# Last feed-forward layer of a four-layer network: dense products ahead of the routing, four batches held in SBUF, one output transfer per batch

## The chip, the cores and the metric

The kernel runs on one core of a Trainium2 chip. The metric is the time of one execution on the device, in microseconds (us); lower is better. The network is one program of four layers (attention, cross-attention, feed-forward in each); the change touches the last sublayer, the store of the result behind it, and nothing else that is computed.

## What is computed

The input is x, 8 batches of 100 tokens of 256 numbers, in fp32. Each of twelve sublayers adds its result to x. The last one is a feed-forward layer with a router:

```python
    def _L3_ffn_ref(x, Wg, bg, We, be):
        probs = jax.nn.softmax(x @ Wg + bg, axis=-1)
        idx = jnp.argmax(probs, axis=-1)
        p = jnp.take_along_axis(probs, idx[..., None], axis=-1)[..., 0]
        e_idx = idx % We.shape[0]
        h = jax.nn.relu(jnp.einsum('bsd,edf->besf', x, We) + be[None, :, None, :])
        onehot = jax.nn.one_hot(e_idx, We.shape[0], dtype=x.dtype)
        out = jnp.einsum('besf,bse->bsf', h, onehot) * p[..., None]
        return out
    x = x + _L3_ffn_ref(_layernorm(x, axis=-1), L3_ffn_Wg, L3_ffn_bg, L3_ffn_We, L3_ffn_be)
```

Wg is 256 by 256, We is 8 experts of 256 by 256, be is 8 by 256. Every token goes through all 8 experts, and one of the 8 results is kept, times the router's probability p.

## The kernel before

The engines run from instruction streams of their own, joined by semaphores. A sublayer is one such block. Behind each stands a barrier of all engines (`end_sublayer`), and nothing of the next begins before it. x stays in SBUF as 100 partitions by 8 batches by 256.

The last sublayer is `l3_ffn`. Its parts, in the order in which they depend on each other:

- The sync engine (SP) issues five loads (L81): `wg`, `bg`, `be`, `iota`, and last `we`, which is 2 MB. All count on one semaphore, `loaded`, and TensorE and VectorE wait for the whole of it.
- VectorE takes the layer norm's statistics (`norm_stats_vector`, L88 to L95) and writes the normed batches `xn` (L106). TensorE meanwhile runs 18 dummy products (`keep_busy`, L113), turns the batches (L3605), and ScalarE copies them to `xt` (L3642). `by_pairs` runs this over two slots, the first pair written out and the other three in a loop on registers.
- Gates: TensorE multiplies each of 8 batches by `wg` (L3615) into two PSUM regions of `summed` in turn. VectorE adds `bg` (L3665), takes the maximum (L3667) and negates it (L3669). ScalarE takes the exponential and its sum (L3648).
- Routing: when all 8 batches are through, VectorE takes the peaks (L3672), their places (L3675), p (L3676, L3679), the expert's number (L3678, L3681) and the one-hot rows `hot` (L3683).
- Dense product: per batch, TensorE fills the four banks of `wide` (L3626), each with two experts' results. The bank of batch b waits until VectorE has read that of batch b - 1 (`z_read`). Batch 0's four banks are filled ahead of the routing. Then TensorE turns `hot` (L3631), ScalarE copies it (L3650), and a small product with `be` gives each token its expert's bias in `summed` (L3634 for batch 0, L3621 for the others).
- Choice: VectorE copies the bias to `acc` (L3689), adds each of 8 experts' results times its one-hot number, each step waiting for the one before (L3694), applies the relu and p (L3700) and adds to x (L3702).

Then follow the barrier and `store` (L247 to L250), one transfer of 800 KB from x to the output.

## Time and profile before

| what | us |
|---|---|
| median of 3 runs | 1530.92 |
| lowest and highest of them | 1526.48, 1542.85 |
| span of the profiled execution | 1546.3 |
| of it, from the start of the last sublayer | 98.6 |

The span runs from the first to the last instruction; for the profiled execution no other time than this span is given. It is longer than each of the three runs, so the differences below are read inside the span and then taken over to the median. PE is TensorE (PEld its weight loads), DVE is VectorE, ACT is ScalarE. A row of the waits says how long an engine stood and who let it go. PEclk, or the granted clock, is 1.0 at 2.4 GHz and 0.5 at 1.2 GHz.

### The profile page before, as it was taken

What the parts mean: (1) busy time and instruction counts of PE and PEld (TensorE: products, weight loads), DVE (VectorE), ACT (ScalarE), POOL (GpSimd) and SP (SyncE); (2) the same over time, 40 slices, a digit from 0 to 9 for tenths busy, and PEclk for the clock granted to TensorE, in tenths of its full rate; (3) what the DMA queues carried; (4) which work ended last, traced back from release to release, by engine and by line L of the source; (5) the groups of instructions that cost most, each with busy time, mean ns of one, the idle gap of its engine ahead of it and who ended that gap; (6) DMA issues with size and microseconds to landing.
All of it is one profiled execution on the core that took longest, in us unless ns stands there. A gap on an engine that the chain in (4) does not pass through costs nothing. (4 is left out here: it accounts for less than half of the span.)

```text
span 1546.3 us, 31598 instructions
## 1 busy us (share of the span) xinstructions
PE 1394.0 (90%) x12524; PEld 1073.6 (69%) x12524; DVE 780.3 (50%) x1747; ACT 640.6 (41%) x1680; POOL 184.2 (12%) x194
## 2 busy tenths in 40 slices
PE   7999999999989899989999768999976896799887
PEld 6776668766556687759999655669974575588632
DVE  3666577665656676500000366610127485477665
ACT  3443226633367266224444235532224684166300
POOL 3000250000034200131111200040023000300000
PEclk9999999999999999999999877999997997799999
DMA  6000240011301200557994100174311000700100
GB/s 209 2 1 1 67 73 10 3 43 40 77 12 20 48 3 3 172 197 262 338 349 172 34 1 22 57 305 150 131 42 53 1 2 1 112 6 3 66 0 22
DMA packets 43944, 120.20 MB, mean 78 GB/s; under 512 B 11931, under 2 KB 28440, under 8 KB 38412
## 3 DMA queue, kind: packets, MB, share of 16 engines
q1 hardware_dynamic: 33048, 62.04, 14.0%
q0 software_dynamic: 7616, 53.12, 9.9%
q10 hardware_dynamic: 3136, 3.03, 0.7%
q8 instruction: 101, 1.65, 0.4%
q14 instruction: 43, 0.35, 0.1%
HBM read 95.78 MB, written 11.00 MB: 69 GB/s over the span
## 5 line engine op out<-in xcount | busy, mean ns | idle before, releaser
L798 PE MATMUL wide<-early_kt,early_q 32*100 32x361 f32 x512 | 107.4, 506 | 2.8 <-PEq L66 1.6
L2528 ACT ACTIVATE l1f_hidden<-wide,l1f_pack 128x128 f32<-128x128 f32 x160 | 58.8, 368 | 78.0 <-PE wide L2467 68.1
L113 PE MATMUL summed<-ident 128*128 128x128 f32 x338 | 51.7, 322 | 37.8 <-PEq L66 37.8
L2630 DVE TENSOR_TENSOR l1f_out<-summed,l1f_pack 128x256 f32<-128x256 f32 x20 | 8.5, 424 | 152.8 <-PE summed L2475 152.8
L113 PEld LDWEIGHTS summed<-ident 128*128 128x128 f32 x338 | 49.1, 234 | 45.3 <-issue 45.3
L2467 PEld LDWEIGHTS wide<-l1f_rt,l1f_pack 128*128 128x128 f32 x640 | 74.5, 192 | 1.8 <-issue 0.8
L2467 PE MATMUL wide<-l1f_rt,l1f_pack 128*128 128x128 f32 x640 | 74.8, 275 | 0.6 <-ACT l1f_rt L2518 0.6
L2475 PE MATMUL summed<-l1f_pack,l1f_hidden 128*128 128x256 f32 x320 | 72.4, 379 | 0.0
L1194 DVE TENSOR_REDUCE l3x_mx<-wide 100x2 f32<-100x722 f32 x64 | 57.8, 907 | 16.5 <-PE wide L798 16.5
L1194 DVE TENSOR_REDUCE l1x_mx<-wide 100x2 f32<-100x722 f32 x64 | 57.8, 907 | 14.0 <-PE wide L798 14.0
L2475 PEld LDWEIGHTS summed<-l1f_pack,l1f_hidden 128*128 128x128 f32 x320 | 59.2, 190 | 7.2
L1194 DVE TENSOR_REDUCE l0x_mx<-wide 100x2 f32<-100x722 f32 x64 | 57.8, 907 | 11.4 <-PE wide L798 11.4
L798 PE MATMUL wide<-late_kt,late_q 32*100 32x361 f32 x256 | 57.3, 540 | 3.7 <-DMA late_q<-l3x_both 3.7
L3626 PE MATMUL wide<-l3f_we,l3f_xt 128*100 128x512 f32 x128 | 59.5, 620 | 1.2 <-DVE l3f_acc L3694 1.2
L2382 POOL DMA_INDIRECT l1f_pack<-l1f_pack_dram,l1f_packi x20 | 18.9, 946 | 255.1 <-DVE l1f_out L2630 129.1
L2973 PE MATMUL wide<-l2f_rt,l2f_w 128*128 128x200 f32 x256 | 46.4, 341 | 0.8 <-ACT l2f_rt L3010 0.8
L3020 ACT ACTIVATE l2f_hidden<-wide 128x200 f32<-128x200 f32 x64 | 21.6, 338 | 61.2 <-PE wide L2973 61.2
L3626 PEld LDWEIGHTS wide<-l3f_we,l3f_xt 128*100 128x100 f32 x128 | 21.7, 174 | 35.1 <-issue 32.2
L2973 PEld LDWEIGHTS wide<-l2f_rt,l2f_w 128*128 128x128 f32 x256 | 45.1, 196 | 1.0 <-issue 1.0
L798 PEld LDWEIGHTS wide<-early_kt,early_q 32*100 32x100 f32 x512 | 32.0, 160 | 19.5 <-issue 10.6
L2951 PE MATMUL summed<-l2f_hidden,l2f_w 128*128 128x200 f32 x256 | 44.8, 333 | 0.0
L1004 ACT ACTIVATE l3x_pt<-turned 121x300 f32<-121x300 f32 x64 | 26.9, 424 | 41.7 <-PE turned L813 41.7
(595 smaller groups left out, 3370.9 us busy)
## 6 DMA issues: line engine op xcount, KB each, us to landing
l2f_w<-l2f_w_dram SPq DMA_DIRECT2D x16, 1024.0 KB, 11.7
ctxt<-ctxt_dram SPq DMA_DIRECT2D x4, 1083.0 KB, 17.3
early_kt<-soon_kd SPq DMA_DIRECT2D x32, 90.8 KB, 3.2
l1f_sorted_x<-l1f_zeros SPq DMA_DIRECT2D x4, 640.0 KB
l1f_rows<-l1f_sorted_x SPq DMA_DIRECT2D x20, 128.0 KB, 7.6
l1f_sorted_y<-l1f_out ACTq DMA_DIRECT2D x20, 128.0 KB
l0f_w<-l0f_w_dram SPq DMA_DIRECT2D x18, 128.0 KB, 2.1
l1f_shared<-l1f_shared_dram SPq DMA_DIRECT2D x1, 2180.0 KB, 8.5
```

The source lines that it names most:

```text
L113: pe.matmul(net.summed[:, 1, 0:P], net.ident[:], net.ident[:], start=True, stop=True)
L798: pe.matmul(wide[0:S, i, 0:SKV], q4[R * i:R * (i + 1), g % 2, b, g // 2, :], kt[R * i:R * (i + 1), g % 2, b, g // 2, 0:SKV], start=True, s ...
L1004: act.activation(pt[:, h % 8], scored[j][0:CH, 0:NCH * S].rearrange("s (c t) -> s c t", c=NCH), ACT.Exp).then_inc(sem["p_ready"], 1)
L1194: dve.tensor_reduce(mx[:, n % 2, :].rearrange("s (i r) -> s i r", r=R)[:, 2 * pair:2 * pair + 2, 0:1], wide[0:S, 2 * pair:2 * pair + 2, 0: ...
L2382: pool.indirect_dma_start(out=pack[:, n % SLOTS, :], out_offset=None, in_=dram["l1f_pack"], in_offset=bass.IndirectOffsetOnAxis(ap=packi[: ...
L2467: last = pe.matmul(wide[:, f % 4, 0:P], w1_of(w, k, f), rt[:, n % 2, k, :], start=k == 0, stop=k == KC - 1)
L2475: last = pe.matmul(summed[:, n % 2, 0:E], hidden[:, f, 0:P], w2_of(w, f), start=f == 0, stop=f == FC - 1)
L2528: act.activation(hidden[:, f, 0:P], wide[:, f % 4, 0:P], ACT.Gelu, bias=b1_of(pack[:, n % SLOTS, :], f)).then_inc(sem["h_ready"], 1)
L2951: last = pe.matmul(summed[:, 0, m * CR:(m + 1) * CR], w2[:, e % SLOTS, f, m * P:(m + 1) * P], hidden[:, f, :], start=f == 0, stop=f == FC - 1)
L2973: last = pe.matmul(wide[:, f % 4, 0:CR], w1[:, e % SLOTS, k, f * P:(f + 1) * P], rt[:, e % 2, k, :], start=k == 0, stop=k == KC - 1)
L3020: act.activation(hidden[:, f, :], wide[:, f % 4, 0:CR], ACT.Gelu).then_inc(sem["h_ready"], 1)
L3626: last = pe.matmul(wide[0:S, n, :], xt[:, k, b, :], we[:, k, n * 512:(n + 1) * 512], start=k == 0, stop=k == KC - 1)
```

## The change

- Loads: SP issues `wg`, `bg`, `we`, and then `iota` and `be`, with a semaphore for each use in place of one for all.
- `xn` has a place for every batch, and the loops on registers are written out. The gates of batches 0 and 1 stand between the turns of x. The gates use four PSUM regions (two of `summed`, two of `turned`). ScalarE loads the table of the exponential before it copies `xt`.
- TensorE goes on from the gates straight into the dense product. Batches 0 to 3 (`HELD`) are copied by ScalarE from `wide` to `held` in SBUF (`hold`), and a bank is free again when it is copied (`z_held`). Batches 4 to 7 are read from PSUM by VectorE as before. The turn of `hot` stands inside batch 1, the bias products inside batches 1 and 2 and then behind each batch; ScalarE copies each bias to `bias`.
- VectorE multiplies `hot` by p once. Each batch is summed in two accumulators (even and odd experts), and these are joined. The relu and the addition to x are one instruction. The bias goes in with the second step; for batch 0 it is added at the end.
- Each batch's x is sent out by SP in a transfer of its own, 100 KB, as soon as it is done; `store` is gone.
- SBUF of the sublayers before (`given`, `late`) is given back ahead of the last one.

```diff
-def store(net):
-    nc = net.nc
-    stored = net.sem("stored")
-    with nc.Block() as block:
-        @block.sync
-        def _(sp):
-            sp.dma_start(net.dram["out"].rearrange("b s d -> s b d"), net.x[:]).then_inc(stored, 16)
-            sp.wait_ge(stored, 16)
...
+    HELD = 4
...
-        pairs = [(wg[:], dram["l3f_wg"]), (bg[:], dram["l3f_bg"].partition_broadcast(S)),
-                 (be[:], dram["l3f_be"]), (iota[:], dram["iota8"]), (we[:], dram["l3f_we"])]
-        n_loaded = 16 * len(pairs)
-        xn = sb("xn", [S, 2, E])
+        xn = sb("xn", [S, B, E])
...
+        held = sb("held", [S, HELD, NE, E])
+        bias = sb("bias", [S, 2, E])
+        acc = sb("acc", [S, 2, 2, E])
...
+        gates = (summed[0:S, 0, 0:E], summed[0:S, 1, 0:E], turned[0:S, 0, 0:E], turned[0:S, 1, 0:E])
...
-                load_weights(sp, net, pairs, sem["loaded"])
+                load_weights(sp, net, [(wg[:], dram["l3f_wg"])], sem["wg_loaded"])
+                load_weights(sp, net, [(bg[:], dram["l3f_bg"].partition_broadcast(S))], sem["bg_loaded"])
+                load_weights(sp, net, [(we[:], dram["l3f_we"])], sem["we_loaded"])
+                load_weights(sp, net, [(iota[:], dram["iota8"]), (be[:], dram["l3f_be"])], sem["be_loaded"])
+                for b in range(B):
+                    sp.wait_ge(sem["x_done"], b + 1)
+                    sp.dma_start(dram["out"][b], net.x[:, b, :]).then_inc(sem["stored"], 16)
+                sp.wait_ge(sem["stored"], 16 * B)
...
+                def gate(b):
+                    pe.wait_ge(sem["xt_ready"], B if b in (2, 3) else b + 1)
+                    if b >= 4:
+                        pe.wait_ge(sem["lg_ready"], b - 3)
+                    for k in range(KC):
+                        last = pe.matmul(gates[b % 4], xt[:, k, b, :], wg[:, k, :], start=k == 0, stop=k == KC - 1)
+                    last.then_inc(sem["g_psum"], 1)
+                def layer(b, n):
+                    u = b * BANKS + n
+                    if b >= 1:
+                        if b <= HELD:
+                            pe.wait_ge(sem["z_held"], u - BANKS + 1)
+                        else:
+                            pe.wait_ge(sem["z_read"], u - BANKS * (HELD + 1) + 1)
+                    for k in range(KC):
+                        last = pe.matmul(wide[0:S, n, :], xt[:, k, b, :], we[:, k, n * 512:(n + 1) * 512], start=k == 0, stop=k == KC - 1)
+                    last.then_inc(sem["z_psum"], 1)
...
+                def shift(b):
+                    if b == 0:
+                        pe.wait_ge(sem["be_loaded"], 32)
+                        pe.wait_ge(sem["ht_ready"], 1)
...
+                        pe.wait_ge(sem["b_ready"], b - 1)
+                    pe.matmul(summed[0:S, b % 2, 0:E], hot_t[:, b, :], be[:], start=True, stop=True).then_inc(sem["b_psum"], 1)
+                for b in range(B):
+                    turn_x(b)
+                    if b == 1:
+                        pe.wait_ge(sem["wg_loaded"], 16)
+                    if b in (2, 4):
+                        gate(b // 2 - 1)
+                for b in range(2, B):
+                    gate(b)
+                pe.wait_ge(sem["we_loaded"], 16)
+                for b in range(B):
                     for n in range(BANKS):
-                        if b >= 1:
-                            pe.wait_ge(sem["z_read"], (b - 1) * BANKS + n + 1)
-                        for k in range(KC):
-                            last = pe.matmul(wide[0:S, n, :], xt[:, k, b, :], we[:, k, n * 512:(n + 1) * 512], start=k == 0, stop=k == KC - 1)
-                        last.then_inc(sem["z_psum"], 1)
-                    if b == 0:
-                        pe.wait_ge(sem["hot_ready"], 1)
-                        for c in range(B):
-                            last = pe.transpose(turned[0:NE, c // 4, (c % 4) * S:(c % 4 + 1) * S], hot[:, c, :], net.ident[0:S, 0:S])
-                        last.then_inc(sem["ht_psum"], 1)
-                        pe.wait_ge(sem["ht_ready"], 1)
-                        pe.matmul(summed[0:S, 0, 0:E], hot_t[:, 0, :], be[:], start=True, stop=True).then_inc(sem["b_psum"], 1)
+                        layer(b, n)
+                        if b == 1 and n == 2:
+                            turn_hot()
+                        if b == 1 and n == 3:
+                            shift(0)
+                        if b == 2 and n == 0:
+                            shift(1)
+                        if b == 2 and n == 2:
+                            shift(2)
+                        if 2 <= b < B - 1 and n == BANKS - 1:
+                            shift(b + 1)
...
+                act.preload_act_table(ACT.Exp)
...
+                def hold(b, n):
+                    act.wait_ge(sem["z_psum"], b * BANKS + n + 1)
+                    act.activation(held[:, b, 2 * n:2 * n + 2, :].rearrange("s e d -> s (e d)"), wide[0:S, n, :], ACT.Copy).then_inc(sem["z_held"], 1)
+                def copy_bias(b):
+                    act.wait_ge(sem["b_psum"], b + 1)
+                    if b >= 2:
+                        act.wait_ge(sem["b_taken"], b - 1)
+                    act.activation(bias[:, b % 2, :], summed[0:S, b % 2, 0:E], ACT.Copy).then_inc(sem["b_ready"], 1)
+                for b in range(B):
+                    copy_xt(b)
+                for b in range(B):
+                    exps(b)
+                for b in range(HELD):
+                    for n in range(BANKS):
+                        hold(b, n)
+                        if b == 1 and n == 2:
+                            act.wait_ge(sem["ht_psum"], 1)
+                            act.activation(hot_t[:].rearrange("e (a b) s -> e a (b s)", a=2), turned[0:NE, :, 0:4 * S], ACT.Copy).then_inc(sem["ht_ready"], 1)
+                        if b == 1 and n == 3:
+                            copy_bias(0)
+                        if b == 2 and n == 0:
+                            copy_bias(1)
+                        if b == 3 and n == 0:
+                            copy_bias(2)
+                for b in range(3, B):
+                    copy_bias(b)
...
-                def normal(b, slot, first):
-                    if not first:
-                        dve.wait_ge(sem["xt_psum"], b - 1)
-                    normalise(dve, net, xn[:, slot, :], b).then_inc(sem["xn_ready"], 1)
-
-                by_pairs(dve, B, normal)
-                dve.wait_ge(sem["loaded"], n_loaded)
+                for b in range(B):
+                    normalise(dve, net, xn[:, b, :], b).then_inc(sem["xn_ready"], 1)
+                dve.wait_ge(sem["bg_loaded"], 16)
                 for b in range(B):
                     dve.wait_ge(sem["g_psum"], b + 1)
-                    dve.tensor_tensor(lg[:, b, :], summed[0:S, b % 2, 0:E], bg[:], ALU.add).then_inc(sem["lg_ready"], 1)
+                    dve.tensor_tensor(lg[:, b, :], gates[b % 4], bg[:], ALU.add).then_inc(sem["lg_ready"], 1)
...
+                dve.wait_ge(sem["be_loaded"], 32)
+                dve.drain()
+                dve.tensor_tensor(hot[:], expert[:].broadcast_to([S, B, NE]), iota[:], ALU.is_equal)
+                dve.drain()
+                dve.tensor_tensor(hot[:], hot[:], p[:].broadcast_to([S, B, NE]), ALU.mult).then_inc(sem["hot_ready"], 1)
+                dve.drain()
+                def expert_of(b, e):
+                    return held[:, b, e, :] if b < HELD else wide[0:S, e // 2, (e % 2) * E:(e % 2 + 1) * E]
+                def choose(b):
+                    one = acc[:, b % 2]
+                    for n in range(BANKS):
+                        if n >= 1:
+                            dve.drain()
+                        if b < HELD:
+                            dve.wait_ge(sem["z_held"], b * BANKS + n + 1)
+                        else:
+                            dve.wait_ge(sem["z_psum"], b * BANKS + n + 1)
+                        for r in range(2):
+                            e = 2 * n + r
+                            if n == 0 and (r == 0 or b == 0):
+                                last = dve.tensor_scalar(one[:, r, :], expert_of(b, e), hot[:, b, e:e + 1], None, ALU.mult)
+                            elif n == 0:
+                                dve.wait_ge(sem["b_ready"], b + 1)
+                                last = dve.scalar_tensor_tensor(out=one[:, r, :], in0=expert_of(b, e), scalar=hot[:, b, e:e + 1],
+                                                                in1=bias[:, b % 2, :], op0=ALU.mult, op1=ALU.add)
+                            else:
+                                last = dve.scalar_tensor_tensor(out=one[:, r, :], in0=expert_of(b, e), scalar=hot[:, b, e:e + 1],
+                                                                in1=one[:, r, :], op0=ALU.mult, op1=ALU.add)
+                        if b >= HELD:
                             last.then_inc(sem["z_read"], 1)
                     dve.drain()
-                    dve.tensor_scalar(one, one, 0.0, p[:, bass.ds(b, 1), :].rearrange("s o e -> s (o e)"), ALU.max, ALU.mult)
+                    if b == 0:
+                        dve.wait_ge(sem["b_ready"], 1)
+                        dve.tensor_tensor(one[:, 1, :], one[:, 1, :], bias[:, 0, :], ALU.add)
+                        dve.drain()
+                    dve.tensor_tensor(one[:, 0, :], one[:, 0, :], one[:, 1, :], ALU.add).then_inc(sem["b_taken"], 1)
                     dve.drain()
-                    dve.tensor_tensor(net.x[:, b, :], net.x[:, b, :], one, ALU.add)
-
-                by_pairs(dve, B, choose)
+                    dve.scalar_tensor_tensor(out=net.x[:, b, :], in0=one[:, 0, :], scalar=0.0, in1=net.x[:, b, :],
+                                             op0=ALU.max, op1=ALU.add).then_inc(sem["x_done"], 1)
+                for b in range(B):
+                    choose(b)
...
-        net.given = Given(net, ctx, "given")
-        with ExitStack() as again:
-            net.context = Context(net, again, "ctxt3")
-            l2_ffn(net)
-        l3_attn(net)
-        net.tiles = RowTiles(net, ctx, "late")
-        cross_attn16(net, "l3x", fresh=True)
+        with ExitStack() as third:
+            net.given = Given(net, third, "given")
+            with ExitStack() as again:
+                net.context = Context(net, again, "ctxt3")
+                l2_ffn(net)
+            l3_attn(net)
+            net.tiles = RowTiles(net, third, "late")
+            cross_attn16(net, "l3x", fresh=True)
         l3_ffn(net)
-        store(net)
```

The lines of the changed kernel are numbered anew: L3612 is the gate, L3623 the dense product, L3639 the bias product, L3679 the copy to `held`, L3685 that to `bias`. On TensorE, this is the stage before, from the turns of x on:

```order
L3605 MATMUL turned<-ident,l3f_xn 128x100 x2
L121 REGISTER_ALU
L121 COMPARE_AND_BRANCH
L3615 MATMUL summed<-l3f_wg,l3f_xt 100x256 x16
L3626 MATMUL wide<-l3f_we,l3f_xt 100x512 x8
L3631 MATMUL turned<-ident,l3f_hot 8x100 x8
L3634 MATMUL summed<-l3f_be,l3f_hot_t 100x256
L3621 MATMUL summed<-l3f_be,l3f_hot_t 100x256
L3626 MATMUL wide<-l3f_we,l3f_xt 100x512 x8
```

And this is the same stretch of TensorE's stream in the changed kernel:

```order
L3604 MATMUL turned<-ident,l3f_xn 128x100 x6
L3612 MATMUL summed<-l3f_wg,l3f_xt 100x256 x2
L3604 MATMUL turned<-ident,l3f_xn 128x100 x4
L3612 MATMUL summed<-l3f_wg,l3f_xt 100x256 x2
L3604 MATMUL turned<-ident,l3f_xn 128x100 x6
L3612 MATMUL turned<-l3f_wg,l3f_xt 100x256 x4
L3612 MATMUL summed<-l3f_wg,l3f_xt 100x256 x4
L3612 MATMUL turned<-l3f_wg,l3f_xt 100x256 x4
L3623 MATMUL wide<-l3f_we,l3f_xt 100x512 x14
L3630 MATMUL turned<-ident,l3f_hot 8x100 x8
L3623 MATMUL wide<-l3f_we,l3f_xt 100x512 x2
L3639 MATMUL summed<-l3f_be,l3f_hot_t 100x256
```

The turn of `hot` stood behind 8 products of the dense layer and now stands behind 14, that is, behind three banks of batch 1 (two products fill a bank). The first bias product stands a bank further on.

On ScalarE, the end of the sublayer was this (`l3f_ex` is the exponential, `l3f_hot_t` the turned one-hot rows):

```order
L3648 ACT_TABLE_LOAD
L3648 ACTIVATE l3f_ex,l3f_sm<-l3f_lg,l3f_ntop 100x256 x8
L3650 ACTIVATE l3f_hot_t<-turned 8x800
```

And it is now this:

```order
L3675 ACTIVATE l3f_ex,l3f_sm<-l3f_lg,l3f_ntop 100x256 x8
L3679 ACTIVATE l3f_held<-wide 100x512 x7
L3696 ACTIVATE l3f_hot_t<-turned 8x800
L3679 ACTIVATE l3f_held<-wide 100x512
L3685 ACTIVATE l3f_bias<-summed 100x256
L3679 ACTIVATE l3f_held<-wide 100x512
L3685 ACTIVATE l3f_bias<-summed 100x256
```

Sixteen copies to `held` and eight to `bias` are new; seven of the sixteen stand ahead of the copy of the turned `hot`, and all of them behind the eight exponentials.

## Rows read from the trace of the kernel before

**Rows 1.** Stretches: us, busy us of each engine, granted clock, DMA share, GB/s.
```profile
0.00:1447.70 1447.70, 1311.90 (x12288) 1036.02 (x12288) 719.19 (x1580) 629.86 (x1652) 184.25 (x194) 0.95 0.26 81
1447.70:1546.30 98.60, 82.09 (x236) 37.58 (x236) 61.15 (x167) 10.71 (x28) 0.00 (x0) 0.90 0.10 34
```
**Rows 2.** Chain that ended last: start, us, what.
```profile
1449.18 8.63 DMA l3f_we<-l3f_we_dram
...
1457.85 4.54 PE summed L3615 x12
...
1478.09 0.69 PE summed L3634 x2
...
1480.41 9.85 PE wide L3626 x16
1490.26 0.60 PE summed L3621 x2
1490.86 7.04 PE wide L3626 x16
...
1529.07 7.05 PE wide L3626 x16
...
1538.08 0.42 DVE x L3702
```
**Rows 3.** Timeline of the last sublayer: start, us, engine, line, instruction, idle before.
```profile
1447.76 2.71 DVE L88 BATCH_NORM_STATS2 stats<-x 100x6 f32<-100x256 f32 x8 [1.15 <-PEq L66]
...
1453.86 0.57 ACT L3642 ACTIVATE l3f_xt<-turned 128x200 f32<-128x200 f32 x2 [2.17 <-PE turned L3605]
...
1466.58 1.08 PE L3615 MATMUL summed<-l3f_wg,l3f_xt 128*100 128x256 f32 x4 [0.36 <-DVE l3f_lg L3665]
...
1467.10 0.41 DVE L3665 TENSOR_TENSOR l3f_lg<-summed,l3f_bg 100x256 f32<-100x256 f32 x1
...
1467.49 7.03 PE L3626 MATMUL wide<-l3f_we,l3f_xt 128*100 128x512 f32 x16
...
1468.18 0.41 DVE L3665 TENSOR_TENSOR l3f_lg<-summed,l3f_bg 100x256 f32<-100x256 f32 x1
...
1476.04 0.23 DVE L3683 TENSOR_TENSOR l3f_hot<-l3f_expert,l3f_iota 100x64 f32<-100x64 f32 x1
...
1476.32 0.85 PE L3631 MATMUL turned<-ident,l3f_hot 100*8 100x100 f32 x8 [1.80 <-DVE l3f_hot L3683]
1477.21 0.83 ACT L3650 ACTIVATE l3f_hot_t<-turned 8x800 f32<-8x800 f32 x1 [7.23 <-PE turned L3631]
...
1539.65 0.31 SPq L250 DMA_DIRECT2D out_dram<-x  x1
```
**Rows 4.** Stretches of 1 us, columns as in rows 1.
```profile
1461.00:1462.00 1.00, 1.00 (x4) 0.66 (x3) 0.82 (x3) 0.08 (x1) 0.00 (x0) 0.50 0.00 0
1462.00:1463.00 1.00, 1.00 (x6) 0.71 (x5) 0.57 (x3) 0.60 (x2) 0.00 (x0) 0.97 0.00 0
...
1480.00:1481.00 1.00, 0.59 (x1) 0.41 (x2) 0.84 (x2) 0.00 (x0) 0.00 (x0) 0.50 0.00 0
...
1486.00:1487.00 1.00, 1.00 (x3) 0.34 (x2) 0.31 (x2) 0.00 (x0) 0.00 (x0) 1.00 0.00 0
```
**Rows 5.** Groups by form: instruction, count, busy us, mean ns, idle before.
```profile
L457 ACT ACTIVATE l0a_v<-wide 100x512 f32<-100x512 f32 x10 | 6.0, 597 | 6.6 <-PE wide L372 6.6
...
L3694 DVE SCALAR_TENSOR_TENSOR l3f_acc<-wide,l3f_hot,l3f_acc 100x256 f32<-100x256 f32 x64 | 30.9, 483 | 16.9 <-PE wide L3626 9.5 <-issue 6.3
L3094 DVE SCALAR_TENSOR_TENSOR x<-l2f_back,l2f_prob,x 100x256 f32<-100x256 f32 x16 | 7.7, 484 | 18.0 <-DMA l2f_back<-sorted_y,l2f_placei 18.0
```
**Rows 6.** Waits of SP's queue: engine, line, releaser, us, times, longest.
```profile
SPq L247 <- DMA out_dram<-x: 5.9, 1, 5.9
```
**Rows 7.** DMA issues: transfer, engine, count, KB each, us to landing.
```profile
early_q<-soon_qt SPq DMA_DIRECT2D x8, 50.0 KB, 2.2
...
early_q<-soon_qt SPq DMA_DIRECT2D x8, 12.5 KB, 1.8
```

More of the change, by code:

```diff
@@ new lines, in turn_hot @@
+                def turn_hot():
+                    pe.wait_ge(sem["hot_ready"], 1)
+                    pe.wait_ge(sem["lg_ready"], B)
+                    for c in range(B):
+                        last = pe.transpose(turned[0:NE, c // 4, (c % 4) * S:(c % 4 + 1) * S], hot[:, c, :], net.ident[0:S, 0:S])
+                    last.then_inc(sem["ht_psum"], 1)
+                def shift(b):
+                    if b == 0:
+                        pe.wait_ge(sem["be_loaded"], 32)
+                        pe.wait_ge(sem["ht_ready"], 1)
+                    if b >= 2:
+                        pe.wait_ge(sem["b_ready"], b - 1)
+                    pe.matmul(summed[0:S, b % 2, 0:E], hot_t[:, b, :], be[:], start=True, stop=True).then_inc(sem["b_psum"], 1)
@@ L3645, in _, with exps @@
[L3645 to L3646 removed]
+                    act.activation(xt[:, :, b, :], turned[:, b % 2, 0:KC * S].rearrange("p (k s) -> p k s", k=KC), ACT.Copy).then_inc(sem["xt_ready"], 1)
+                def exps(b):
                     act.wait_ge(sem["top_ready"], b + 1)
                     act.activation(ex[:, b, :], lg[:, b, :], ACT.Exp, bias=ntop[:, b, :], accum_out=sm[:, b, :]).then_inc(sem["ex_ready"], 1)
[L3649 removed]
```

44 lines of the change are left out of this document (6 added, 38 removed).

## The prediction

> **What bounds the kernel now.** I read the stretches first. The last sublayer and the store take 98.6 us of the 1546.3 us span [rows 1]; the 1447.7 us ahead of them run the same instructions in both kernels, so they cancel. Then I read the chain that ended last [rows 2]. It passes from the load of `we` to TensorE, through VectorE's routing, and from 1480.41 to 1536.12 it is TensorE alone: batches of 7.04 us with 0.60 us of bias product between them. So the dense product on TensorE bounds the sublayer, and time is won only where TensorE stands, where it runs at half clock, and ahead of and behind it. The timeline [rows 3] and the clock by microseconds [rows 4] show these places:
>
> - The gates. TensorE starts them at 1457.85, when `we` is in, though the first copies of x are done at 1454.43 (1453.86 + 0.57). The first 12 passes take 4.54 us, 1.51 a batch; a batch at full clock takes 1.08 [rows 2, 3]. The clock is 0.50 at 1461 and back at 0.97 at 1462 [rows 4]. The last gate ends at 1467.66.
> - The routing. Batch 0 ends at 1474.52 (1467.49 + 7.03). Then TensorE stands 1.80 us for `hot`, turns it, stands 0.9 us for ScalarE's copy, does 1.2 us of bias products and stands until 1480.41 for VectorE's first bank. After that the clock is 0.50 until it is 1.00 again at 1486 [rows 4], and batch 1 takes 9.85 us where the next takes 7.04.
> - The end. VectorE is done at 1538.50, SP issues the store at 1539.65 and then stands 5.9 us for it, to 1545.86 [rows 2, 3, 6]. The span ends 0.4 us later.
>
> **The change part by part.**
>
> *Gates ahead.* `wg` no longer waits for `we`, and the gates of batches 0 and 1 stand between the turns. The first can start once two batches are copied and the third is turned, near 1454.6. Two gates (2.16 us) and the next two turns fill TensorE until about 1457.2. Three turns and their copies remain, some 0.45 us each since a copy is 0.29 (0.57 for two), so the six other gates start near 1458.6 and, at 1.08 each, end near 1465.1. That is 2.5 us earlier. VectorE keeps up: it also needs 1.08 a batch (1468.18 less 1467.10 [rows 3]). The bounds: no gain if the gates end where they did; 3.6 us if they follow without any wait. A fall of the clock to half over four gates would cost 4 x 0.43 = 1.7 us of the 2.5. The table load that moved ahead of the copies lies beside the norm's steps, where ScalarE idles 2.17 us before its first copy [rows 3]; if it did not fit there, it would delay the copies by no more than that, 2.2 us.
>
> Of the clock the row says that after the turns, with TensorE waiting on copies, it fell to 0.50. The Trainium skill (TensorE: Matmul & The Clock Gate, Loop structure matters more than you think) says that matmuls kept back to back stay at the full clock, and that copying results out does not break this. By that rule the gates stay at 2.4 GHz and the sum holds; by the row they may still fall. I keep the fall as a rival.
>
> *Dense product without the gap.* From the last gate on TensorE has 8 batches x 7.04, 8 bias products x 0.60 and one turn of `hot` of 0.85: 56.3 + 4.8 + 0.85 = 62.0 us. Before, the same stretch is 1467.66 to 1536.12, 68.5 us. So 6.5 us go, the waits (3.7) and the half clock (2.8), and TensorE ends near 1465.1 + 62.0 = 1527.1. For this, three waits must stay covered:
>
> - Bank free. A copy to `held` of 100 x 512 is like `l0a_v`, 597 ns [rows 5]; a bank is filled in 7.04 / 4 = 1.76. ScalarE starts them after its last exponential, near 1467.4, when one bank is full, and has caught up a bank later. Sixteen copies are 9.6 us beside 28 us of TensorE. If the cover were gone, each copy would cost up to 0.6 us on TensorE.
> - `hot` ready. From the last logits (1468.18) to `hot` (1476.27) are 8.1 us, and the new product with p is one more of 0.23 with its drain, 0.3. With the last logits near 1465.2, `hot` is there at 1473.6. TensorE asks at 1465.1 + 7 banks x 1.76 = 1477.4. The wait of 1.80 is covered by 3.8 us. Queued behind it are all later banks, so each us beyond these 3.8 costs one.
> - ScalarE's copy of the turned `hot` (0.83) lies beside bank (1, 3) of 1.76.
>
> *VectorE's late start.* This is the wait that the change adds. `choose(0)` ends with the bias, which stands behind bank (1, 3) at about 1480.1, the bias product 0.7 and its copy. VectorE has `hot` at 1473.6, is through the eight experts by 1478, stands until about 1481.2, and ends batch 0 at 1482.8. Behind this wait stand batches 1 to 7. A step is 0.48 us by itself, and 0.58 with what it stood by issue ((30.9 + 6.3) / 64 [rows 5]); ten steps a batch are 4.8 to 5.8 us. Reading from SBUF gains nothing: with all operands there a step is 484 ns against 483 from PSUM [rows 5]. I take 4.9, near the lower end, because only every second step now waits for the one before. So batches 1 to 3 are done at 1497.5 (1500.2 at 5.8). TensorE fills (4, 0) at about 1498.9 and needs it read at 1504.8. VectorE has caught up either way, and this part costs nothing.
>
> *The end of the chain.* Behind the last bank stood two steps, the relu and the addition, 2.38 us. Now they are two steps of which one does not wait, the join and the relu with the addition: 2.1, a gain of 0.3 (0 to 0.5).
>
> *The output.* Seven transfers lie beside TensorE's batches, 7.64 us apart. The last is 100 KB. The nearest rows are 1.8 us at 12.5 KB and 2.2 at 50 KB [rows 7], and the 800 KB took 0.31 + 5.9 = 6.2; a line between the last two gives 2.5 at 100 KB. I take 2.2. What stood ahead of the store, the sublayer's barrier, now stands behind it: VectorE's gap at such a seam is 1.15 us [rows 3]. So from VectorE's end to the span's end there are 0.1 + 2.2 + 1.15 = 3.45 us instead of 7.8, a gain of 4.3. Bounds: 5.5 (1.8 us and only the 0.4 of before behind it), and zero (6.2 us and 1.5 behind).
>
> The Trainium skill speaks against this edit (DMA: Bandwidth & Descriptors, Rules for kernel authors): many small transfers should be put together into one large. By its estimate in Anatomy of one DMA, 2.0 us and bytes / 436e3, eight of 100 KB are 17.9 us and one of 800 KB is 3.9. By the sum of all the change would lose; but only the last of the eight is on the chain, 2.2 by that estimate. No row shows a 100 KB store alone.
>
> *Sum.* 2.5 + 6.5 + 0.3 + 4.3 = 13.6 us, so a span of 1532.7. The profiled span, 1546.3, is 1.0% above the median of the runs; the edits do not scale with the rest, so I take 13.6 from the median: 1530.92 - 13.6 = 1517.3, or 0.89% less.
>
> **The rivals.**
>
> 1. *The clock falls in the gates, or the store lands late* (gain 10 to 12). For it: the fall in rows 4 came after turns like these, and no row has the small store. Against: TensorE's waits there shrink. With the fall alone the gain is 13.6 - 1.7 = 11.9; with a transfer of 4 us (midway to 6.2) it is 11.8; with both 10.1. Time 1519 to 1521.
> 2. *All at the good end* (gain 15.8). The gates end 1.1 us earlier and the end takes 2.3 instead of 3.45: 1515.1, just beyond 1%.
> 3. *VectorE becomes the bound*, the one that ends on the other side. Its place is batches 1 to 7, where it reads `held` while ScalarE writes it and SP's transfers read x. It begins at 1482.8 and may end at 1529: 6.6 us a batch before it bounds. From 6.6 + 13.6 / 7 = 8.5 us a batch, 0.85 a step, the kernel is slower than before; to be slower by 1% it takes 10.7. At 1.1 us a step: 7 x 4.4 = 31 us more, a time of 1548. Against it: 484 ns in rows 5.
> 4. *The edit does not advance the gates* (gain 11.1), since the turns go by ScalarE's copies as before and VectorE paces the rest: 1519.8.
>
> **How the numbers follow.** About 1% is what a measurement of this kernel can tell from no change; the three runs lie 1.1% apart. The forecast (gain 12 to 15) has 0.5, rivals 1 and 4 together 0.32, rival 2 has 0.14 and rival 3 0.04. The forecast's 0.89% and the spread of the runs put 0.22 of its 0.5 beyond 1%; rival 2 gives 0.09, rivals 1 and 4 give 0.06. Faster 0.37; slower 0.03, of rival 3; the same 0.60. The range is from 1507 (rival 2 and a median 0.5% low) to 1529 (a gain of 10 and a median 0.5% high).
>
> **What would show it.** In the profile of the changed kernel TensorE's dense product should run without a stand from the last gate on, at a granted clock of 1.00, 62 us long; the clock should not be 0.50 near the turn of `hot`. VectorE should stand once, some 3 us, for ScalarE's bias copy in batch 0, and later only for banks. The last gate should end 17.4 us after the sublayer's start at 1447.7 (before 20.0), and SP should wait about 2 us for the last transfer. The forecast is wrong if TensorE waits for `z_held` or `z_read`, if the whole dense product is longer than 64 us, or if the end from VectorE's last instruction takes over 5 us.

## The result, and the profile of the changed kernel

| | before | changed |
|---|---|---|
| median, 20 runs each, us | 1529.33 | 1515.44 |
| lowest and highest run | 1519.96, 1542.85 | 1506.88, 1529.28 |
| span of the profiled execution | 1546.3 | 1527.5 |
| of it, the last sublayer and the store | 98.6 | 83.0 |

The ratio is 0.9938 with an interval of 0.9914 to 0.9961; the medians stand as 0.9909. The profiled execution of the changed kernel took 1529.28 us around its span of 1527.5. By the bound of 1% this is no change that counts, though the interval lies below 1 altogether. The forecast was 1517.3 us, with 0.60 for within 1%. The 20 runs of the changed kernel lie in two groups, six at 1527.2 to 1529.3 us and fourteen at 1506.9 to 1517.4, and the profiled execution is one of the six.

The stretches of the changed kernel, split where its last sublayer begins (columns as in [rows 1]); the last line is a part of the one above it, from the last gate to the last bank:

```profile
0.00:1444.55 1444.55, 1317.76 (x12288) 1043.97 (x12288) 720.32 (x1580) 630.40 (x1652) 184.49 (x194) 0.94 0.26 81
1444.55:1527.50 82.95, 76.62 (x236) 35.65 (x236) 55.37 (x161) 22.63 (x52) 0.00 (x0) 0.98 0.13 41
...
1460.52:1522.35 61.83, 61.82 (x152) 22.96 (x151) 41.68 (x114) 14.71 (x31) 0.00 (x0) 1.00 0.04 12
```

The last sublayer is 15.6 us shorter, and TensorE is busy for 92% of it instead of 83%. In the dense product it is busy for 61.82 of 61.83 us at a granted clock of 1.00, which is the sign that the prediction named. The other 3.2 us between the two spans lie ahead of it, in instructions that are the same. The chain that ended last shows how it now goes:

```profile
1444.60 5.88 PE summed L113 x36
...
1455.10 1.97 PE turned L3612 x8
1457.07 1.73 PE summed L3612 x8
1458.79 1.73 PE turned L3612 x8
1460.52 12.02 PE wide L3623 x28
1472.54 0.69 PE turned L3630 x8
1473.22 1.72 PE wide L3623 x4
...
1515.30 7.05 PE wide L3623 x16
...
1523.87 0.43 DVE x L3770
```

It is nearly TensorE alone. Where [rows 2] had the load of `we`, VectorE's routing and a batch of 9.85 us, there is now one piece of 12.02 us that runs over the end of batch 0 into batch 1 (28 passes, 0.43 us each, the full clock). The two pieces that the routing fed, VectorE's chain and ScalarE's copy, are gone from the chain. What the engines waited for in this sublayer:

```profile
ACT l3f_held L3679 <- PE wide L3623: 17.3, 14, 1.9
...
DVE l3f_acc L3756 <- ACT l3f_bias L3685: 5.7, 3, 4.4
...
DVE l3f_acc L3766 <- ACT l3f_bias L3685: 2.0, 1, 2.0
```

ScalarE waits for banks and no bank waits for ScalarE. VectorE's new wait for the bias of batch 0 is the 2.0 us; the row above it holds one that the prediction had not seen, 4.4 us in batch 2. And the wait of SP's queue that answers to [rows 6]:

```profile
SPq L3583 <- DMA out_dram<-x: 1.6, 1, 1.6
```

In the table below each profile is cut at four marks. All times are us from the start of the last sublayer (SP's first load of it). "Ahead" is what the profile shows before that, the same instructions in every kernel.

| profile | ahead | last gate ends | from there to the last bank | to VectorE's end | to the span's end | sublayer |
|---|---|---|---|---|---|---|
| before | 1447.7 | 19.95 | 68.45 | 2.39 | 7.80 | 98.6 |
| changed | 1444.6 | 15.97 | 61.82 | 1.96 | 3.20 | 83.0 |
| before, again | 1429.5 | 20.50 | 68.22 | 2.41 | 7.74 | 98.9 |
| changed, again | 1423.6 | 15.12 | 61.83 | 1.96 | 3.21 | 82.1 |
| store alone | 1435.4 | 18.60 | 67.70 | 2.39 | 3.21 | 91.9 |
| one store | 1424.4 | 15.98 | 61.82 | 1.96 | 7.54 | 87.3 |
| gap filled | 1423.2 | 19.81 | 65.90 | 2.40 | 7.83 | 95.9 |
| hot early | 1444.0 | 15.97 | 65.05 | 1.96 | 3.18 | 86.2 |
| semaphores alone | 1421.1 | 18.63 | 67.94 | 2.39 | 7.78 | 96.7 |
| gates behind | 1443.0 | 15.89 | 61.83 | 1.96 | 3.19 | 82.9 |
| two regions | 1424.2 | 17.02 | 61.82 | 1.96 | 3.17 | 84.0 |
| held one | 1443.2 | 15.97 | 65.56 | 1.95 | 3.26 | 86.7 |
| slow choice | 1432.7 | 15.98 | 65.74 | 4.19 | 3.16 | 89.1 |
| fewer dummies | 1444.0 | 15.04 | 61.82 | 1.96 | 3.21 | 82.0 |

### The profile page after: what moved, and what is told of

It is laid out like the page before. It is cut to its first block and busy times, and to the rows that moved or that the text cites. A ratio compares the mean times of both kernels' runs of the same rounds, so it can differ in the third digit from the quotient of the medians.

```text
span 1527.5 us, 31428 instructions
## 1 busy us (share of the span) xinstructions
PE 1394.4 (91%) x12524; PEld 1079.6 (71%) x12524; DVE 775.7 (51%) x1741; ACT 653.0 (43%) x1704; POOL 184.5 (12%) x194
## 5 line engine op out<-in xcount | busy, mean ns | idle before, releaser
L788 PE MATMUL wide<-early_kt,early_q 32*100 32x361 f32 x512 | 112.6, 532 | 2.8 <-PEq L66 1.6
L3623 PE MATMUL wide<-l3f_we,l3f_xt 128*100 128x512 f32 x128 | 57.2, 597 | 0.0
L994 ACT ACTIVATE l1x_pt<-turned 121x300 f32<-121x300 f32 x64 | 26.9, 424 | 40.6 <-PE turned L803 40.6
```

The costliest lines, as they stand in the source:

```text
L788: pe.matmul(wide[0:S, i, 0:SKV], q4[R * i:R * (i + 1), g % 2, b, g // 2, :], kt[R * i:R * (i + 1), g % 2, b, g // 2, 0:SKV], start=True, s ...
L994: act.activation(pt[:, h % 8], scored[j][0:CH, 0:NCH * S].rearrange("s (c t) -> s c t", c=NCH), ACT.Exp).then_inc(sem["p_ready"], 1)
L3623: last = pe.matmul(wide[0:S, n, :], xt[:, k, b, :], we[:, k, n * 512:(n + 1) * 512], start=k == 0, stop=k == KC - 1)
```

## How finely the kernel can be measured, and the two kernels again

Both kernels were run again without an edit.

> The kernel before, unchanged, measured against itself. Both theories: a ratio of 1.000, and its interval and the scatter of its runs say how finely this kernel can be measured. The last sublayer's stretch (from SP's first load of it to the end of the span) takes 98.6 us again within 0.5 us, while the stretch ahead of it varies by several us from one profile to the next.

Measured: 1530.05 us against 1530.10, a ratio of 0.999 (0.9952 to 1.0028), and 98.9 us in the sublayer. The runs of this one kernel lie between 1521.66 and 1546.11 us. The expectation held.

> The changed kernel, unchanged. Theory A (the change acts in the last sublayer alone): that stretch takes 83.0 us again within 0.5 us, 15.6 less than before, and the ratio is about 0.990 with an interval that holds 1 - 15.6/1530 = 0.9898. Rival B (a part of the 15.6 us is given back ahead of the last sublayer, for which the first ratio of 0.9938 speaks): the ratio is 0.993 to 0.995 again, and the stretch ahead of the sublayer is 4 to 6 us longer than in the profiles of the kernel before.

Measured: 1511.54 us (six runs), a ratio of 0.9874 (0.9824 to 0.9924), and 82.1 us in the sublayer. The two ratios of the same kernel, 0.9938 and 0.9874, lie on either side of 1 - 15.6/1530 = 0.9898, and their intervals overlap between 0.9914 and 0.9924. Rival B expected 0.993 to 0.995 and a longer stretch ahead; that stretch was 1423.6 us, shorter than in any but two of the five profiles of the kernel before and its variants. It is not excluded for a part of the gain: the stretch ahead averages 1436.0 us over the nine profiles of the changed kernel and its variants and 1431.4 over the five others, a difference well inside its scatter. That the sublayer was 0.8 us under the expected is its start: here the clock was 1.00 from the first microsecond, while it was 0.50 for some 3.4 us of the dummy products in all the others, and the last gate ended 0.85 us earlier.

The stretch ahead explains the scatter. It ran from 1421.1 to 1447.7 us over 14 profiles of the same instructions. Two profiles of it show one of the places (columns as in [rows 1]). This is the kernel before:

```profile
900.00:960.00 60.00, 44.52 (x203) 29.68 (x204) 41.50 (x109) 26.57 (x59) 0.11 (x1) 0.75 0.05 14
```

And this is the same stretch of "semaphores alone":

```profile
900.00:960.00 60.00, 50.06 (x350) 32.49 (x351) 45.07 (x153) 33.23 (x82) 0.11 (x1) 0.89 0.06 15
```

The granted clock is 0.75 in one and 0.89 in the other, and TensorE gets 203 and 350 instructions done. Against a scatter of 26 us the change's 15.6 are small, so the terms below are read in the sublayer, where the two profiles of each kernel agree within 0.9 us. The kernels behind these terms have one profile each.

## The output

> The kernel before with the output part of the change alone. Theory A: the parts add up, so the stretch from VectorE's last instruction to the end of the span falls from 7.8 to 3.2 us as in the changed kernel, the last sublayer from 98.6 to 94.0, and the ratio is 0.997. Rival C (the small transfers cost something ahead of the end): the dense product or the choice gets longer than before, and less than 4.6 us is won.

```diff
+                for b in range(B):
+                    sp.wait_ge(sem["x_done"], b + 1)
+                    sp.dma_start(dram["out"][b], net.x[:, b, :]).then_inc(sem["stored"], 16)
+                sp.wait_ge(sem["stored"], 16 * B)
...
-                    dve.tensor_tensor(net.x[:, b, :], net.x[:, b, :], one, ALU.add)
+                    dve.tensor_tensor(net.x[:, b, :], net.x[:, b, :], one, ALU.add).then_inc(sem["x_done"], 1)
...
-        store(net)
```

Measured: the end is 3.21 us instead of 7.8, as expected, and so are the waits: 1.6 us for the last transfer, as in the changed kernel. The ratio is 0.9945 (0.9917 to 0.9974), whose interval holds the 0.997 that 4.6 us make. The sublayer is 91.9 us and not 94.0. Rival C is out, since nothing got longer; the other 2.1 us are in the gates (18.60 instead of 19.95) and in the dense product behind them (67.70 instead of 68.45). The clock did not fall in the gates of this profile. It did in the two profiles of the kernel before and in "gap filled", and not in this one and in "semaphores alone", though the gates are the same in all five, and so are the stands of TensorE between the turns ahead of them (0.68, 0.58 and 0.57 us within 0.02). So of the kernel before's sublayer some 1.3 us in the gates, and 2 us with what follows, come and go from one execution to the next.

> The changed kernel with one transfer of 800 KB when all batches are done, in place of eight of 100 KB. Theory A: the wait for the last transfer is the 5.9 us of the kernel before and not 1.6, so the sublayer takes 83.0 + 4.3 = 87.3 us. Rival D (the gain lies in the barrier that stood ahead of the store, not in the size of the transfer): 1.1 us or less is lost, 84.1 us.

```diff
-                for b in range(B):
-                    sp.wait_ge(sem["x_done"], b + 1)
-                    sp.dma_start(dram["out"][b], net.x[:, b, :]).then_inc(sem["stored"], 16)
-                sp.wait_ge(sem["stored"], 16 * B)
+                sp.wait_ge(sem["x_done"], B)
+                sp.dma_start(dram["out"].rearrange("b s d -> s b d"), net.x[:]).then_inc(sem["stored"], 16)
+                sp.wait_ge(sem["stored"], 16)
```

Measured: 87.3 us, to the tenth what theory A said. The wait of SP's queue in this kernel:

```profile
SPq L3583 <- DMA out_dram<-x: 5.9, 1, 5.9
```

It is 5.9 us as in [rows 6]. So 4.3 us come from the size of the last transfer, and rival D is out. The barrier, which only moved from one side of the store to the other, is worth the small rest: 7.54 us at the end here and 7.80 before.

## The gap of the routing, and the half clock behind it

> The kernel before with 17 dummy products on TensorE where it stood for the routing: 8 ahead of the turn of hot, 4 behind it, 5 behind the first bias product. The waits stay. Theory A (the half clock of batch 1 is the price of the gap, 2.8 us, and separate from the gap's 3.8 us): the granted clock stays at 1.00 through batch 1, which takes about 7.1 us instead of 9.85, and the sublayer takes 98.6 - 2.8 = 95.8 us. Rival E (the clock falls there whatever TensorE does): no change, 98.6.

```diff
+                def fill(count):
+                    for _ in range(count):
+                        pe.matmul(summed[:, 1, 256:256 + P], net.ident[:], net.ident[:], start=True, stop=True)
...
                     if b == 0:
+                        pe.wait_ge(sem["lg_ready"], B)
+                        fill(8)
                         pe.wait_ge(sem["hot_ready"], 1)
...
                         last.then_inc(sem["ht_psum"], 1)
+                        fill(4)
                         pe.wait_ge(sem["ht_ready"], 1)
...
+                        fill(5)
```

Measured: 95.9 us in the sublayer. Its chain behind the last gate:

```profile
1442.97 6.87 PE wide L3629 x16
1449.83 1.78 PE summed L3602 x16
...
1451.63 0.85 PE turned L3636 x8
1452.48 0.92 PE summed L3602 x8
1453.40 0.67 PE summed L3640 x2
1454.07 1.31 PE summed L3602 x10
1455.38 0.60 PE summed L3624 x2
1455.98 7.04 PE wide L3629 x16
```

L3602 are the dummies. Batch 1 begins 13.0 us behind the last gate (1442.97 to 1455.98), 12.8 before (1467.66 to 1480.41 [rows 2, 3]), so the gap is all there. But the batch takes 7.04 us and not 9.85, and the granted clock is 1.00 from the last gate on. The half clock is 2.8 us by itself, and it comes from TensorE's stands in the gap, since it is gone when they are filled. Rival E is out.

> The changed kernel with the turn of hot back behind batch 0, so that TensorE waits for the routing again, but not for ScalarE's copy nor for VectorE's first bank. Theory A: batch 0 ends 7.0 us behind the last gate, hot is there 2.9 us later, so TensorE stands 2.9 us, and the sublayer takes 83.0 + 2.9 = 85.9 us if the clock holds. Rival F (any stand of this size drops the clock): 2.8 us more, 88.7.

```diff
-                        if b == 1 and n == 2:
+                        if b == 0 and n == 3:
                             turn_hot()
```

(and the same place for ScalarE's copy of the turned `hot`.) Measured: 86.2 us. TensorE's wait in this kernel:

```profile
PE turned L3630 <- DVE l3f_hot L3735: 3.1, 1, 3.1
```

It stood 3.1 us in one piece, and the clock stayed at 1.00. So rival F is out for this stand. But the length of a stand does not decide: in "store alone" the clock fell behind one of 1.79 us, at the end of `hot`'s turn:

```profile
1462.65 0.85 PE L3635 MATMUL turned<-ident,l3f_hot 100*8 100x100 f32 x8 [1.79 <-DVE l3f_hot L3687]
```

```profile
1463.00:1464.00 1.00, 0.50 (x6) 0.26 (x3) 0.00 (x0) 0.46 (x1) 0.00 (x0) 0.74 0.00 0
1464.00:1465.00 1.00, 0.58 (x2) 0.44 (x3) 0.00 (x0) 0.36 (x1) 0.00 (x0) 0.50 0.00 0
```

In "semaphores alone" it fell half a microsecond later, with the same stand ahead of it. In both profiles of the kernel before it fell behind the second stand, of 0.9 us, and ahead of the third. What decides is not shown. The 3.2 us that this edit costs are what the later place of the turn is worth.

## The gates

> The kernel before with a semaphore for each load and the loads in the new order, but the gates behind all turns as before. Theory A (the gates are won by standing between the turns, so that TensorE is busy and its clock holds): the gates start at most 0.3 us earlier, since the last turn ends when we lands, the clock falls as before, and 0.3 us or less is won. Rival G (they are won by no longer waiting for we): 2 us or more.

```diff
-                load_weights(sp, net, pairs, sem["loaded"])
+                load_weights(sp, net, [(wg[:], dram["l3f_wg"])], sem["wg_loaded"])
+                load_weights(sp, net, [(bg[:], dram["l3f_bg"].partition_broadcast(S))], sem["bg_loaded"])
+                load_weights(sp, net, [(we[:], dram["l3f_we"])], sem["we_loaded"])
+                load_weights(sp, net, [(iota[:], dram["iota8"]), (be[:], dram["l3f_be"])], sem["be_loaded"])
...
-                pe.wait_ge(sem["loaded"], n_loaded)
+                pe.wait_ge(sem["wg_loaded"], 16)
```

Measured: 96.7 us, and the gates start at 10.01 us, against 10.14 before and 9.97 in "store alone", which kept the old semaphore. So with the turns as they were, the load of `we` is not what holds the gates: the turns end just when it lands. Theory A was right in that. The match is close, though. In the second profile of the kernel before the load landed later, and the gates, which start at 10.69 there, did wait for it:

```profile
1440.22 8.37 PE L3615 MATMUL summed<-l3f_wg,l3f_xt 128*100 128x256 f32 x28 [0.67 <-DMA l3f_we<-l3f_we_dram]
```

Of the 1.9 us that the sublayer is shorter, 1.3 are the clock, which did not fall in the gates of this profile: the last gate ends at 18.63 here and at 18.60 in "store alone". The rest is in the dense product (67.94 instead of 68.45).

> The changed kernel with the gates of batches 0 and 1 behind the turns. Theory A: TensorE has only the turns to do beside ScalarE's copies; 1.7 us of gates move behind them, and the clock falls to 0.50 for about 3 us as it did before, 1.3 us more: 83.0 + 3.0 = 86.0 us. Rival H (the clock holds all the same, since the turns are no longer in a loop): 1.7 us, 84.7.

```diff
-                    if b == 1:
-                        pe.wait_ge(sem["wg_loaded"], 16)
-                    if b in (2, 4):
-                        gate(b // 2 - 1)
-                for b in range(2, B):
+                pe.wait_ge(sem["wg_loaded"], 16)
+                for b in range(B):
                     gate(b)
```

Measured: 82.9 us, no loss at all. Both theories failed here, and with them the reason that I had given for this part. The chain of this kernel:

```profile
1448.96 0.19 PE turned L3604 x2
...
1452.02 1.73 PE summed L3612 x8
1453.74 1.73 PE turned L3612 x8
1455.47 1.73 PE summed L3612 x8
1457.20 1.73 PE turned L3612 x8
1458.92 12.02 PE wide L3623 x28
```

With the turns written out, and a place in `xn` for every batch, the turns are paced by ScalarE's copies and the gates start 8.8 us into the sublayer, not 10.0; two gates between them push the other turns back by as much as they take. And eight gates back to back take 7.1 us (1451.85 to 1458.92, counting the start that overlaps the last copy), 0.87 us a batch, where I had reckoned with 1.08.

> The kernel with the gates behind the turns (82.9 us in the last sublayer), now with two PSUM regions for the gates as before, not four. Theory A (the change's gain in the gates comes from the four regions, which let TensorE go at its own 0.88 us a batch, and from the loop written out): TensorE is paced by VectorE at 1.08 us, the eight gates take 8.6 us as in the kernel before at full clock instead of 7.1, and the sublayer takes 84.4 us. Rival I (the clock alone made the gates faster): no change, 82.9.

```diff
-                    if b >= 4:
-                        pe.wait_ge(sem["lg_ready"], b - 3)
+                    if b >= 2:
+                        pe.wait_ge(sem["lg_ready"], b - 1)
                     for k in range(KC):
-                        last = pe.matmul(gates[b % 4], xt[:, k, b, :], wg[:, k, :], start=k == 0, stop=k == KC - 1)
+                        last = pe.matmul(gates[b % 2], xt[:, k, b, :], wg[:, k, :], start=k == 0, stop=k == KC - 1)
```

Measured: 84.0 us. The chain of this kernel shows why:

```profile
1433.21 2.63 PE summed L3612 x12
...
1435.85 1.08 PE summed L3612 x4
...
1436.93 1.08 PE summed L3612 x4
```

Three batches go at TensorE's own pace, and each of the other five waits until VectorE has read a region, 1.08 us. The gates take 8.2 us instead of 7.1. This is 0.4 less than theory A said, because only five gates are paced and not all; its mechanism is shown, and rival I is out: the clock was 1.00 in both.

So the 4.0 us of this part, against the profile of before, are made of 1.2 us for the earlier start of the gates (8.82 instead of 10.0), 1.1 for the four regions, and 1.3 for the clock in those profiles where it fell. A rest of 0.4 is not assigned. The place between the turns has no share. The 1.2 us are not split: the loop written out, the places of `xn` and the semaphore of its own for `wg` came together. The last of these is worth nothing by itself, but it may be needed for them: in the two profiles of the kernel before, `we` landed 10.1 and 10.6 us into the sublayer, and gates that wait for it could not have started at 8.82. No run has the turns written out with one semaphore for all loads.

## Batches held, and VectorE's cover

> The changed kernel with one batch held in SBUF instead of four (HELD = 1), the bias product of batch 1 moved ahead of batch 2 for it. Theory A (TensorE only has to get past the routing, and VectorE is then faster than TensorE): TensorE stands once, about 2.3 us ahead of batch 2, until VectorE has read bank (1, 0), and the sublayer takes 83.0 + 2.3 = 85.3 us. Rival J (all four must be held, since VectorE starts late and stays behind): TensorE stands in batches 2 to 4 as well, 5 us or more, 88 us or above.

```diff
-    HELD = 4
+    HELD = 1
```

(with the bias product of batch 1 ahead of batch 2, and ScalarE's copies in that order.) Measured: 86.7 us, 3.8 more than the changed kernel. TensorE in this kernel:

```profile
1473.48 1.10 PE L3639 MATMUL summed<-l3f_be,l3f_hot_t 8*100 8x256 f32 x4
1476.90 7.09 PE L3623 MATMUL wide<-l3f_we,l3f_xt 128*100 128x512 f32 x12 [2.31 <-DVE l3f_acc L3749]
```

The stand is the 2.3 us that were expected, and it is the only one. The rest is the half clock behind it: the next 12 passes take 7.09 us where 12 of the full clock take 5.3, and the granted clock is 0.50 for 3.4 us. Stand and half clock are 4.1 us together; the 0.3 by which the loss is smaller are not assigned. I had left the price of the clock out of the number. Rival J is out: one batch held is enough to pass the routing, and the other three save this one stand and the fall behind it.

> The changed kernel with four more steps of VectorE in each of batches 1 to 7 whose result nobody reads, 0.56 us each. Theory A (VectorE's cover is about 8.7 us, the time for which it still waits for banks from batch 4 on, and it then becomes the bound): seven batches of 5.2 + 2.24 = 7.4 us from 1477.4 of the changed kernel's profile end near 1530, so the sublayer takes 83.0 + 5.5 = 88.5 us. Rival K (each batch has its own cover of 7.64 - 5.2 = 2.4 us, which the four steps fit in): 83.0, or 2.2 us more for the last batch alone, 85.2.

```diff
+                    for _ in range(4 if b >= 1 else 0):
+                        dve.scalar_tensor_tensor(out=spare[:, 0, :], in0=one[:, 0, :], scalar=hot[:, b, 0:1],
+                                                 in1=one[:, 1, :], op0=ALU.mult, op1=ALU.add)
+                        dve.drain()
```

Measured: 89.1 us, 6.1 more. That this is near theory A's 88.5 is luck, since the way there is another. 2.2 us are in the last batch (4.19 instead of 1.96 behind the last bank), and 3.9 in the middle: one stand of TensorE of 2.15 us, and behind it a batch of 8.81 us instead of 7.04, with the granted clock at 0.50 for 3.4 us of it. The chain of this kernel there:

```profile
1487.61 0.40 issue
1488.00 0.48 DVE l3f_spare L3770
...
1490.36 8.81 PE wide L3624 x16
...
1499.76 7.04 PE wide L3624 x16
```

VectorE bounds up to batch 5, which must wait until bank (4, 0) is read; from there on its 7.0 us a batch are less than TensorE's 7.64 and it bounds no more. So both theories held half: there is a cover for the late start, which these four steps overran once, and one for each batch, which they did not. The first is the small one: in the changed kernel VectorE was through with bank (4, 0) at 1497.88 and TensorE came to it again at 1500.02, 2.1 us later. The second is what VectorE waited for banks from batch 5 on, 8.7 us in all:

```profile
DVE l3f_acc L3759 <- PE wide L3623: 7.6, 9, 0.8
...
DVE l3f_acc L3753 <- PE wide L3623: 1.1, 2, 0.6
```

## A version that goes a little further

> The kernel with the gates behind the turns, with 14 dummy products ahead of the turns instead of 18. In the changed kernel the first normed batch is there about 1 us before TensorE is through with them. Theory A: the turns start about 1.0 us earlier, the clock is up by then, and the sublayer takes 81.9 us; as the last version it should have a ratio of about 0.989 to the kernel before. Rival L (with four fewer the clock is not up when the turns begin, or falls between them): 83 us or more.

```diff
-                keep_busy(pe, net, 18)
+                keep_busy(pe, net, 14)
```

(on top of "gates behind".) Measured: 82.0 us in the sublayer, 0.9 less than the changed kernel, a ratio to the kernel before of 0.9895 (0.9855 to 0.9936) and a median of 1515.13 us over six runs. Its chain passes from the norm's statistics to the turns, no longer through the dummies:

```profile
1448.26 2.36 DVE l3f_xn L106 x7
1450.63 0.37 PE turned L3604 x2
```

Rival L is out in the sublayer. Against the kernel before this version's interval lies below 1. Whether it is faster than the changed kernel the whole time cannot say, since 0.9 us is far inside the scatter. The profiles say it only where the clock is at 0.50 in the dummy products, as it was here: the changed kernel's second profile, with the clock at 1.00 there, took 82.1 us with all 18.

## Why the prediction was right, and where its steps were not

**The number.** Forecast: 13.6 us less. The medians moved by 13.9 us. The first ratio, taken at 1530 us, says 9.5 (6 to 13), the second 19; the sublayer's own profile says 15.6. The chances put 0.60 on within 1%, where the first ratio is, and 0.37 on faster. The second measurement would have fallen to the other. So that 13.6 and 13.9 agree is partly luck, and inside the sublayer the forecast was 2.0 us short: the gates gave 1.5 us more than forecast (4.0, also beyond the stated bound of 3.6), the output 0.3 more, the dense product and the end of the chain 0.1 each. The 15.6 us are near rival 2's 15.8, but that had its excess over the forecast in the gates and the end about alike (1.1 and 1.15). Whether a fraction of the 15.6 us is given back ahead of the sublayer was not settled: its stretch there scatters more than the change moves it.

**Dense product without the gap.** Forecast 62.0 us from the last gate to the last bank, 61.8 measured. "Gap filled" shows the half clock in it (2.8 us), and "hot early" what a stand for the routing costs (3.2 us). All three covered waits held. `hot` was there at 25.84 us, forecast 25.9. The cover of the turn was 2.0 us and not 3.8, because the gates that came earlier brought TensorE to the turn earlier too, while VectorE, which goes at 1.08 a batch, gained less.

**Gates ahead.** This step failed in its reason and its size: the forecast was 17.4 us for the last gate, measured 15.97. "`wg` no longer waits for `we`" was worth nothing by itself, because another wait ended at the same time, the turns themselves; "the gates stand between the turns" was worth nothing either. What brought the start forward, the turns written out with their places in `xn`, the text does not price. "At 1.08 each" was a row read as TensorE's pace, though it was VectorE's ([rows 3] has a stand of 0.36 us for VectorE in that very row); the four regions, which the text does not weigh at all, lifted it to 0.87.

**The clock in the gates.** It was the first rival, with the fall in [rows 4] for it. In none of the nine profiles of kernels with the written-out turns did it fall there; in those with the loop it fell in three of five. The Trainium skill's rule that matmuls kept back to back hold the full clock (TensorE: Matmul & The Clock Gate, Loop structure matters more than you think) does not settle this: in the kernel before the clock fell 0.8 us into gates that ran back to back, behind turns with stands between them, and in two profiles with the same turns it did not fall. The stands between the written-out turns are shorter, some 0.3 us; that they are the reason is not shown.

**VectorE's late start.** The stand for batch 0's bias was 2.0 us, forecast 3.2 (from 1478 to 1481.2). The prediction had batches 1 to 3 done 49.8 us into the sublayer; they were done at 52.5. The step that failed is that it looked for the bias only in batch 0: the copy of batch 2's bias stands behind the first copy of batch 3 on ScalarE, and VectorE waited 4.4 us for it. It cost nothing, since VectorE was through with bank (4, 0) 2.1 us before TensorE came to it again, and had caught up by batch 5. In the prediction VectorE stood ready 1.4 us before that bank was full (1497.5 and 1498.9); in the run it came to it 2.9 us after (1497.0 and 1494.1). "Slow choice" shows how near it was: 2.2 us more a batch overran it.

**Reading from SBUF.** The steps with three operands took 481 ns from `held` and 479 from PSUM, as [rows 5] had said. Only the first step of a batch, with one tensor, got shorter, 349 ns against 483.

**The end of the chain.** 1.96 us, forecast 2.1. Behind the last bank stood four instructions and not two, since the two steps of the last bank's experts belong to the 2.38 us as well; the difference is not touched by that. **The output.** 3.20 us, forecast 3.45; the transfer took 0.29 + 1.6 = 1.9 us, forecast 2.2, near the row of 12.5 KB. The Trainium skill's rule to put small transfers together (DMA: Bandwidth & Descriptors, Rules for kernel authors) does not hold for a transfer that ends the program: "one store" followed it and was 4.3 us slower. By the Trainium skill's estimate (the same page, Anatomy of one DMA), which it states for transfers that GpSimd issues, 100 KB take 2.2 us and 800 KB 3.9; for these stores, issued by SP, the runs show 1.9 and 6.2, so the first is near and the second is not.

## What to carry to other kernels

When a resource is waited for, look at what else would be late at the same moment before pricing its removal; the early load brought nothing alone, and the cheapest edit of this change, two more PSUM regions, brought 1.1 us. A stand of TensorE costs what it lasts and, in six of the seven profiles here that had one behind the last gate, 1.6 to 2.8 us more of half clock in the batch behind it, so useful work that can be put there can count double. And at the end of a program only the last transfer is on the path, so send what is done early and keep the last piece small.

## What the runs showed of the hardware that was not expected

A store of 100 KB took 1.9 us from issue to the semaphore and one of 800 KB 6.2, so 700 KB more cost 4.3 us, 167 GB/s by 1 KB rows. A stand of TensorE of 3.1 us in one piece ("hot early") left the granted clock at 1.00, while one of 1.79 us ("store alone"), one of 2.15 ("slow choice") and one of 2.3 ("held one") were followed by the fall to 0.50. And the same instructions ahead of the sublayer took between 1421.1 and 1447.7 us on one core in 14 profiles, with granted clocks of 0.75 and 0.89 in the same 60 us.
